# A rebuilt prologue: input order, a power on GpSimd, selection products, one exchange for the median

## The reference

```python
x = x + g(xn) * xn            # xn = _gn(x): 32 groups of 16 channels, normalised
# with xf = xn as (b, c, 256)
mean, mx, std = xf.mean(-1), xf.max(-1), xf.std(-1, ddof=1)
u   = stack([mean, mx, std], axis=-1)           # (8, 512, 3)
med = median(u.reshape(b, -1), axis=-1)         # one median of 1536 values per image
z   = einsum('bck,ck->bc', (u - med) ** 3, cfc_w) / sqrt(1 + 1e-5) * bn_w + bn_b
g   = sigmoid(z)
```

## Time and profile before

| | before |
|---|---|
| median of 3 runs | 725.55 us |
| profiled execution, its own time | 728.12 us |
| span of the profile | 726.4 us |
| PE busy | 646.2 us (89%) |
| DVE busy | 441.0 us (61%) |
| ACT busy | 336.2 us (46%) |
| POOL busy | 285.7 us (39%) |

### The profile page before, as it was taken

How to read it: one execution, slowest core, us unless ns; L and a number is a source line. 1 busy time by engine, 2 the same in 40 slices (tenths; PEclk the granted TensorE clock), 3 DMA queues, 4 the chain that set the end, 5 groups by cost and what they waited for, 6 DMA issues and landing times.

```text
span 726.4 us, 14162 instructions
## 1 busy us (share of the span) xinstructions
PE 646.2 (89%) x4944; PEld 543.8 (75%) x4945; DVE 441.0 (61%) x974; ACT 336.2 (46%) x616; POOL 285.7 (39%) x329
## 2 busy tenths in 40 slices
PE   0213989999999999999999999999899999999992
PEld 0203978888888888888689899999687878878881
DVE  7775344756565656573645996233567677767771
ACT  8641254646464646464634223434444544544440
POOL 1340153434343434342421113865454554545524
PEclk9999999999999999999999999999999999999996
DMA  9800000101010101020025433352856556555543
GB/s 309 328 0 0 1 2 1 60 2 58 0 58 0 58 0 58 0 73 16 31 86 234 131 117 117 116 173 73 302 90 114 95 107 110 98 110 103 103 70 43
DMA packets 24786, 62.61 MB, mean 86 GB/s; under 512 B 3056, under 2 KB 7920, under 8 KB 23216
## 3 DMA queue, kind: packets, MB, share of 16 engines
q1 hardware_dynamic: 14912, 41.69, 16.0%
q0 software_dynamic: 9168, 20.45, 15.5%
q10 hardware_dynamic: 672, 0.03, 0.1%
HBM read 39.09 MB, written 23.07 MB: 86 GB/s over the span
## 4 chain that ended last, share of the span: by engine, by line
PE 59%; DMA 26%; DVE 7%; issue 3%; POOL 3%; ACT 1%; SPq 0%; DVEq 0%; POOLq 0%; ACTq 0%
PE PS L1554 25%; DMA out_tokens<-yo,dest 24%; PE scores L1554 12%; PE PS L1663 6%; PE scores L1826 5%; PE scores L1649 3%; PE PS L1614 2%; DMA T<-in_x 1%; PE PS L1603 1%; DMA out_tokens<-yo,dest_halves 1%; DVE front L1034 1%; DVE qT L960 1%; POOL w_l L528 1%; PE PS L1690 1%; DVE qT L961 1%
## 5 line engine op out<-in xcount | busy, mean ns | idle before, releaser
L1554 PE MATMUL scores<-xb,sw_h 128*128 128x256 f32 x512 | 94.2, 284 | 0.0
L647 POOL DMA_INDIRECT out_tokens<-yo,dest x36 | 57.5, 1598 | 79.1 <-DMA out_tokens<-yo,dest 77.3
L1554 PEld LDWEIGHTS scores<-xb,sw_h 128*128 128x128 f32 x512 | 80.9, 191 | 2.3 <-ACT probs L745 0.4
L1554 PE MATMUL PS<-xt_h,w_h 128*128 128x256 f32 x256 | 76.2, 298 | 1.5 <-DVE xt_l L1176 1.5
L552 POOL TENSOR_SCALAR_AFFINE_SELECT probs<-probs 128x256 f32<-128x256 f32 x128 | 52.0, 432 | 57.6 <-ACT probs L749 56.8
L1554 PE MATMUL PS<-xt_l,w_h 128*128 128x256 f32 x256 | 73.9, 289 | 0.0
L1554 PE MATMUL PS<-xt_h,w_l 128*128 128x256 f32 x256 | 73.7, 288 | 0.0
L1554 PE MATMUL scores<-xb,sw_l 128*128 128x256 f32 x256 | 72.3, 282 | 0.0
L1191 DVE RECIPROCAL rden<-PS 128x256 f32<-128x256 f32 x32 | 56.2, 1755 | 24.8 <-PE PS L1663 24.8
L1554 PE MATMUL scores<-wgu_h,xgT_h 128*128 x156 | 64.8, 416 | 2.0 <-DVE xgT_l L1516 2.0
L745 ACT ACTIVATE probs<-scores 128x768 f32<-128x768 f32 x64 | 51.4, 802 | 26.8 <-PE scores L1649 26.7
(11 more groups left out here) (297 smaller groups left out, 1597.1 us busy)
## 6 DMA issues: line engine op xcount, KB each, us to landing
wgu_l<-in_wgu SPq DMA_DIRECT2D x8, 1024.0 KB, 6.6
T<-in_x SPq DMA_DIRECT2D x8, 512.0 KB, 7.7
w_in<-in_wqkvo SPq DMA_DIRECT2D x4, 1024.0 KB, 12.5
x_rows<-x SPq DMA_DIRECT2D x8, 512.0 KB, 2.8
x_cols<-x2T SPq DMA_DIRECT2D x8, 512.0 KB, 2.6
xc<-x_cols SPq DMA_DIRECT2D x8, 512.0 KB, 3.3
out_tokens<-T SPq DMA_DIRECT2D x8, 512.0 KB, 7.5
wd_sb<-in_wd SPq DMA_DIRECT2D x8, 512.0 KB, 7.0
```

Of the source, the lines that this page charges most:

```text
L647: pool.indirect_dma_start(out[:, :], bass.IndirectOffsetOnAxis(dest[:, t:t + 1], 0), yo[:, t % 3, :], None, compute_op=ALU.add).then_inc(y ...
L1554: ins = pe.matmul(out, lhs(k, a), rhs(k, b), start=m == 0, stop=m == len(products) - 1)
```

## The change

- The images are loaded, and DVE takes their statistics, in the order 0, 1, 4, 2, 5, 3, 6, 7. ACT works in two groups, images 0 and 1 and then 2 and 3, each with its sums, scaling and squares.
- ACT's square root and the five DVE instructions behind it go. POOL raises both variances to a power in one instruction (128x64, exponents -0.5 and 0.5). DVE forms u with three small instructions.
- u is widened to 16 columns for each image (the spare ones hold a large number) and transposed in one piece; DVE copies the transposed matrix from PSUM. Twelve float32 products with a 0/1 matrix `selection`, which POOL fills ahead of the power, put the values where the twelve transposes put them.
- The last steps of the median are done in one exchange: each partition finds the least value at or above `low`, the greatest up to a bound `high`, the least above it, and a count; one product brings the four to 8 rows, a second one spreads the median.
- The coefficients take fewer instructions: the two channel weights are multiplied beforehand, and one over (1 + exp) is taken together with the deviation.
- ACT applies the coefficients to two of the four pieces of image 0.
- PE gets products whose result nobody reads (`keep_busy`): 10 before the group means, 8 before the transpose of u, 9 before the transposes of image 0 and 16 behind them.
- POOL's low parts of the weights no longer wait for `spread_full`.

```diff
+UM = 16
+ARRIVAL = (0, 1, 4, 2, 5, 3, 6, 7)
...
+        exponents = kf[:, 20 * n32:22 * n32]
+        deviation = kf[:, 22 * n32:23 * n32]
+        u_wide = vf[:, 0:B * UM]
+        u = u_wide.rearrange("p (b n) -> p b n", b=B)[:, :, 0:UP]
+        uw = vf[:, B * UM:B * UM + 3 * B * UP].rearrange("p (k n) -> p k n", k=3)
+        uT = vf[:, 416:416 + P]
...
-            for b in range(B):
+            for b in ARRIVAL:
...
+            pool.tensor_copy(selection.rearrange("p (n b j) -> p n b j", n=UP, b=B),
+                             ident[:, :].rearrange("p (b n) -> p n b", b=B)[:, 0:UP, :].unsqueeze(3).to_broadcast(
+                                 [P, UP, B, THRESHOLDS])).then_inc(selection_ready, 1)
+            pool.wait_ge(var_ready, 1)
+            pool.tensor_tensor(root, var2, exponents, ALU.pow).then_inc(root_ready, 1)
...
+            for first, group in enumerate(((0, 1), (2, 3))):
+                these = [(b, k, CB * b + k) for b in group for k in range(CB)]
+                lo, hi = CB * group[0], CB * (group[-1] + 1)
+                for b, k, c in these:
+                    act.wait_ge(x_loaded[b], 16)
+                    ins = act.activation(unread[c], at(T, b)[:, k * S:(k + 1) * S], ACT.Copy,
+                                         accum_out=small[:, 12, c:c + 1])
+                ins.then_inc(act_sums, 1)
...
-            act.wait_ge(var_ready, 1)
-            act.activation(root, var2, ACT.Sqrt).then_inc(root_ready, 1)
...
+            act.wait_ge(coef_ready, 1)
+            for k in (2, 3):
+                ins = act.activation(front[:, k * S:(k + 1) * S], at(T, 0)[:, k * S:(k + 1) * S], ACT.Identity,
+                                     bias=coefB[:, k:k + 1], scale=coefA[:, k:k + 1])
+            ins.then_inc(y0_upper, 1)
...
-            dve.wait_ge(dve_step, step_of(dve.reciprocal(inv2, root)))
-            dve.wait_ge(dve_step, step_of(dve.tensor_tensor(root2, var2, inv2, ALU.mult)))
-            dve.wait_ge(dve_step, step_of(dve.tensor_tensor(root2, root2, root, ALU.add)))
-            dve.wait_ge(dve_step, step_of(dve.reciprocal(inv2[:, 0:n32], root2[:, 0:n32])))
-            r = inv2[:, n32:2 * n32]
-            dve.wait_ge(dve_step, step_of(dve.tensor_scalar(r, inv2[:, 0:n32], 2.0, None, ALU.mult)))
-            u3 = u.rearrange("p (n k) -> p n k", k=UK)
-            def spread_out(k):
-                return every_u[k].rearrange("p (c b j) -> p b c j", c=CB, b=B)
-            def every(t):
-                return t.rearrange("p (b c) -> p b c", b=B).unsqueeze(3).to_broadcast([P, B, CB, THRESHOLDS])
-            dve.tensor_tensor(spread_out(0), every(K(7)), every(r), ALU.mult).then_inc(every_ready, 1)
-            dve.tensor_tensor(spread_out(1), every(K(10)), every(r), ALU.mult).then_inc(every_ready, 1)
-            dve.tensor_tensor(spread_out(2), every(root2[:, n32:2 * n32]), every(inv2[:, 0:n32]),
-                              ALU.mult).then_inc(every_ready, 1)
-            dve.tensor_tensor(u3[:, :, 0], K(7), r, ALU.mult)
-            dve.tensor_tensor(u3[:, :, 1], K(10), r, ALU.mult)
-            dve.scalar_tensor_tensor(u3[:, :, 2], root2[:, n32:2 * n32], 0.5, r, ALU.mult, ALU.mult).then_inc(u_ready, 1)
+            by_b = "p (b n) -> p b n"
+            r = root[:, 0:n32]
+            u4 = u.rearrange("p b (c k) -> p b c k", k=UK)
+            def per_batch(t):
+                return t.rearrange(by_b, b=B)
+            dve.wait_ge(dve_step, n.value())
+            dve.tensor_tensor(u4[:, :, :, 0], per_batch(K(7)), per_batch(r), ALU.mult)
+            dve.tensor_tensor(u4[:, :, :, 1], per_batch(K(10)), per_batch(r), ALU.mult)
+            dve.tensor_tensor(u4[:, :, :, 2], per_batch(root[:, n32:2 * n32]), per_batch(r),
+                              ALU.mult).then_inc(u_ready, 1)
...
+            dve.wait_ge(uT_full, 1)
+            dve.tensor_copy(uT, PS[6][:, 0:P]).then_inc(uT_ready, 1)
+            dve.wait_ge(uT_ready, 1)
...
+            size_step = step_of(dve.scalar_tensor_tensor(low_size, low, -1.0, low, ALU.mult, ALU.max))
+            from_low = step_of(dve.tensor_scalar(least_of[:, 0, :], uT, low, BIG, ALU.is_lt, ALU.mult))
+            dve.wait_ge(dve_step, size_step)
+            dve.wait_ge(dve_step, step_of(dve.tensor_scalar(low_size, low_size, 3.0 / 2 ** 23, WIDTHS[-1], ALU.mult,
+                                                            ALU.add)))
+            high_step = step_of(dve.tensor_tensor(high, low_size, low, ALU.add))
+            step_of(dve.tensor_tensor(least_of[:, 0, :], least_of[:, 0, :], uT, ALU.add))
+            dve.wait_ge(dve_step, high_step)
+            counted = step_of(dve.tensor_scalar(least_of[:, 2, :], uT, high, 0.0, ALU.is_le, ALU.add,
+                                                accum_out=cols[:, 3:4]))
+            over_high = step_of(dve.tensor_scalar(least_of[:, 1, :], uT, high, BIG, ALU.is_gt, ALU.mult))
+            dve.wait_ge(dve_step, counted)
+            step_of(dve.scalar_tensor_tensor(least_of[:, 2, :], least_of[:, 2, :], BIG, uT, ALU.mult, ALU.add))
+            dve.wait_ge(dve_step, over_high)
+            dve.wait_ge(dve_step, step_of(dve.tensor_tensor(least_of[:, 1, :], least_of[:, 1, :], uT, ALU.subtract)))
+            dve.wait_ge(dve_step, step_of(dve.tensor_reduce(cols[:, 0:3], least_of, AX.X, ALU.min)))
+            dve.tensor_tensor(cols_of, cols.unsqueeze(2).to_broadcast([P, 4, UM]),
+                              own_slot.unsqueeze(1).to_broadcast([P, 4, UM]), ALU.mult).then_inc(med_in, 1)
...
+            by_slot = PS[4][0:B, 384:384 + 4 * UM].rearrange("p (k j) -> p k j", k=4)
+            at_low, minus_high, over, count, apart, second, both = [rows[:, k:k + 1] for k in range(7)]
+            dve.wait_ge(dve_step, step_of(dve.tensor_reduce(count, by_slot[:, 3, :], AX.X, ALU.add)))
+            step_of(dve.tensor_reduce(rows[:, 0:3], by_slot[:, 0:3, :], AX.X, ALU.min))
+            dve.wait_ge(dve_step, step_of(dve.tensor_scalar(apart, count, MED_N / 2 + 0.5, BIG, ALU.is_lt, ALU.mult)))
+            dve.wait_ge(dve_step, step_of(dve.scalar_tensor_tensor(second, at_low, apart, over, ALU.add, ALU.min)))
+            dve.wait_ge(dve_step, step_of(dve.tensor_tensor(both, second, minus_high, ALU.subtract)))
+            dve.tensor_scalar(diagonal, ident[0:B, 0:B], both, 0.5, ALU.mult, ALU.mult).then_inc(med_in, 1)
...
-                uw[:, 0, :].rearrange(by_b, b=B), uw[:, 2, :].rearrange(by_b, b=B),
-                prm[:, 0:UP].unsqueeze(1).to_broadcast([P, B, UP]), ALU.mult)))
-            dve.wait_ge(dve_step, step_of(dve.tensor_reduce(
-                K(11), uw[:, 0, :].rearrange("p (n k) -> p n k", k=UK), AX.X, ALU.add)))
-            bn_scale = float(1.0 / np.sqrt(np.float32(1.0) + np.float32(EPS)))
-            dve.wait_ge(dve_step, step_of(dve.scalar_tensor_tensor(
-                K(12).rearrange(by_b, b=B), K(11).rearrange(by_b, b=B), bn_scale,
-                prm[:, UP:UP + CB].unsqueeze(1).to_broadcast([P, B, CB]), ALU.mult, ALU.mult)))
...
+            squared = step_of(dve.tensor_tensor(uw[:, 1, :], uw[:, 0, :], uw[:, 0, :], ALU.mult))
...
+                uw[:, 2, :].rearrange(by_b, b=B), uw[:, 0, :].rearrange(by_b, b=B),
+                weights3.unsqueeze(1).to_broadcast([P, B, UP]), ALU.mult)))
...
+            dve.wait_ge(dve_step, step_of(dve.scalar_tensor_tensor(K(0), K(15), 1.0, deviation, ALU.add, ALU.mult)))
+            dve.wait_ge(dve_step, step_of(dve.reciprocal(K(2), K(0))))
             step_of(dve.tensor_scalar(coefA[:, :], K(2), 1.0, None, ALU.add))
-            dve.wait_ge(dve_step, step_of(dve.scalar_tensor_tensor(
-                coefB[:, :], grp_mean, -1.0, K(2), ALU.mult, ALU.mult)))
+            dve.scalar_tensor_tensor(coefB[:, :], grp_mean, -1.0, K(2), ALU.mult, ALU.mult).then_inc(coef_ready, 1)
...
-                for k in range(CB):
+                for k in range(2 if isinstance(b, int) and b == 0 else CB):
...
+            def keep_busy(times):
+                for _ in range(times):
+                    pe.matmul(PS[3][:, 384:512], ident[:, :], ident[:, :], start=True, stop=True)
+            pe.wait_ge(consts_done, NCONSTS)
+            pe.wait_ge(x_loaded[B - 2], 16)
+            keep_busy(10)
...
+            keep_busy(8)
+            pe.wait_ge(u_ready, 1)
+            pe.transpose(PS[6][:, 0:P], u_wide, ident[:, :]).then_inc(uT_full, 1)
+            pe.wait_ge(selection_ready, 1)
+            pe.wait_ge(uT_ready, 1)
...
+                ins = pe.matmul(spread_u[q // (UP // 2)][:, at_q:at_q + P], selection[:, q * P:(q + 1) * P], uT,
+                                start=True, stop=True)
...
+            pe.matmul(PS[4][0:B, 384:384 + 4 * UM], own_batch, cols_of.rearrange("p k j -> p (k j)"), start=True,
+                      stop=True).then_inc(med_out, 1)
...
+            pe.matmul(PS[6][:, 0:B], ones[0:B, :], diagonal, start=True, stop=True).then_inc(med_out, 1)
...
+            keep_busy(9)
             y_transposes("lead", 0, 0)
```

(32 more changed lines are left out.)

141 lines of the change are left out of this document (44 added, 97 removed).

## The result

The changed kernel takes 737.56 us (median of 6 runs, 736.42 to 739.93), the kernel before 725.77 on the same chip (6 runs, 724.23 to 728.19). The ratio is 1.0162, with an interval of 1.0137 to 1.0188: slower by 1.6%, where 720.9 us were forecast. The profiled execution took 737.16 us, its span is 735.4.

A forecast was written before the change was run, and what follows sets the result against it. Step latency was taken to bound the prologue, and PE to be full from the first projection on. Terms -1.0 + 2.8 - 2.8 - 0.65 - 0.45 - 2.6 = -4.7 us on 725.55 gave 720.9; range 715.5 to 727.5.

The forecast's parts named there:

- From the variances to the first round: Prologue from the variances to the first count: 8.5 us instead of 5.65, so 2.8 us more than before.
- the products: Twelve float32 products with `selection` on PE ahead of the rounds: 4.0 us, between 2.8 and 5.3 by the clock.
- The power: POOL's 128x64 power on the path to u: 3.0 us, the geometric middle of 0.7 and 13.1.
- Rival D: POOL's power goes by column, 13.1 us on the path: +6.8 us, 732.3 us; deciding from 10 us on; chance 0.08.
- The low pieces beside DVE: POOL's low parts of the weights, now started before the rounds, beside DVE instructions: contention noted, nothing added.
- the counts: DVE's counts in the rounds beside POOL's low parts: they read PSUM, so nothing added; eight rounds of 2.17 us unchanged.
- The median: Exchange of the median after the rounds: 5.7 us instead of 8.5, a gain of 2.8 us.
- the coefficients: Coefficients after the median: three instructions fewer on the path and one square overlapped, a gain of 0.65 us.
- The affine: Affine pieces of image 0, two on ACT at 0.4 to 0.5 us each: 1.0 us instead of 1.39, gain 0.45.
- The order of x: Image order in DVE's statistics: the last maximum ends at 20.0 us instead of 21.0, a gain of 1.0 us.
- Hidden up to 16 us: POOL's filling of `selection` between 4 and 21 us: hidden, at no cost, up to 16 us of work.
- The clock: PE's clock, raised by unread products, at first transposes, second transposes and first projections: 2.6 us credited of 4.2 possible.

The follow-up runs named there:

- e9: e5 with five more powers of 4 to 64 columns on POOL, results unread, run once for its profile: 732.74 us.
- e2: Changed kernel with the root back on ACT with five DVE instructions and the low pieces waiting: 725.10 us, 0.9936 of the kernel before.
- e1: Changed kernel with POOL's low pieces waiting again for the end of the twelve products, power kept: 734.44 us, 1.0064 of the kernel before.
- e3: e2 with POOL's low pieces started as soon as ACT's root is there: 734.22 us, 1.0054 of the kernel before.
- e12: e1 with five more small DVE instructions beside the power, results unread, run once for its profile: 733.81 us.
- e4: Kernel before with one line changed, POOL's low pieces started when the root is there: 739.26 us, 1.0116 of the kernel before.
- e5: e2 with POOL's copy into `selection` moved behind DVE's first constants: 726.19 us, 0.9909 of the kernel before.
- e11: e5 unchanged, measured again beside e10: 724.53 us, 0.9914 of the kernel before.
- e7: e5 with only the 9 and 16 unread products behind the median kept: 726.64 us, 0.9921 of the kernel before.
- e8: e5 with the images in the old order 0 to 7: 725.93 us, 0.9925 of the kernel before.
- e10: e5 with 6 more unread products between the second transposes and the projections, other counts slightly shifted: 725.96 us, 0.9929 of the kernel before.
- e6: e5 without any of the unread products: 727.49 us, 0.9936 of the kernel before.

## Why the prediction was wrong

**The step that failed** is "From the variances to the first round", forecast at 8.5 us and measured at 24.76. Of the 16.3 us between them 15.8 are two errors, and each has its runs; 0.3 more are the products, at 4.27 for 4.0.

*The power, 7.6 us.* I took 3.0 where it is 10.59, inside my bounds of 0.7 and 13.1. The middle was argued from what a long routine might overlap; the surplus of 0.4 us on two columns was the only measurement, and half of it, 0.2 us a column, was closer than my value (0.158, e9). e2 against e1 shows 9.3 us for the power against ACT's root. Rival D had this mechanism, and its point, from p = 10 on, is met; but I gave it 0.08. The sum with p = 10.59 and nothing else changed is -4.7 + 7.6 = +2.9 us. e1, which has just this, gives +4.2, of which 1.3 are its products at 5.34 us instead of 4.0.

*The low pieces beside DVE, 8.2 us, priced at nothing.* This is a wait that the sum did not have. I saw that "POOL's low parts now start before the rounds" and weighed them against the counts, which read PSUM. That part holds: L1056 takes 1.02 to 1.03 us beside the low pieces at 50.14, as in the rounds without them. But the pieces start with the power's end, together with the three instructions that form u, and I did not price those. Three at 2.3 us instead of 0.2 are 6.5; the fourth makes the copy 1.7 later. The Trainium skill (GPSIMD Engine Reference, 8) says that GpSimd and DVE contend where a DVE instruction has two SBUF inputs or is in a 2-port perf mode; it gives no size. The trace agrees: all four have two SBUF inputs, and each waits for a whole POOL instruction. Whether the one-input TENSOR_SCALAR of e3 (1.83 us) was in such a mode no trace here shows; beside the power two inputs did not wait (e9, e12). e1, e3 and e4 show the cost three times, at 7.6, 9.1 and 9.0 us, in three different prologues. Neither error alone makes the measured result: e1 is the power alone (+0.64%), e3 the pieces alone (+0.54%). Over e2, which has neither (-0.64%), they are 1.3% and 1.2%; together from there that would be +1.8%, and +1.6% was measured.

**The other terms** were right or small. The median gained 3.7 for 2.8 and the coefficients 0.64 for 0.65. The affine gained 0.2 for 0.45: ACT's two pieces end at 74.20 (I put them at 0.4 to 0.5 us each, they take 0.54), and the nine unread products, at the low level throughout, at 74.47, so the transposes wait some 0.2 us for them. The order of x gained 0.45 for 1.0. "Hidden up to 16 us" was wrong of `selection`: it held a conversion at 4.01 for 1.3 us, of which 0.2 reach the end (e5). Most of the rest is the third image, which came at 8.31 in e5 and not at 8.02. The clock gave all of the 4.2 us in this execution, where I credited 2.6; e5 and e11 show that it is not given every time, and that part of it can go at the next pause. Which of the two this execution would show was luck. That the clock column before "reads 0.50 only at 97 to 100 us" was misread: it is down at 356 to 360 us too (0.52 and 0.62); nothing in the sum hangs on it.

With both errors out the rest of the sum holds in size. e2 is 5.2 us faster than before by the medians (interval of the ratio 0.9915 to 0.9956, so 3.2 to 6.2 us); the forecast was 4.7. That its first count is at 31.91, where 31.8 was forecast, is luck: the variances end 1.25 us late there (24.55 for 23.3), and the step behind them takes 7.36 us for 8.5, since ACT's root and its five instructions take 2.1 us where the sum has 3.1 up to u, and the products take 3.21 for 4.0. The clock also gave e2 more than the 2.6 of the sum: its 96 projections take 11.74 us. e5's kernel, measured twice, has the lowest ratios: 0.9909 and 0.9914, about 6.5 us below before and 2.5% below the changed kernel's ratio. The intervals of e2, e7, e8 and e10 overlap them.

**Still open:** what in POOL's instructions holds DVE; how much each group of unread products is worth in the whole time (e6, e7 and e10 differ by less than their intervals); and why the clock falls at one pause in one execution and at another in the next.

## What to carry to other kernels

When a step is moved off an engine, look at what stood behind its old wait: here the low pieces, not the power alone, came to lie beside the path. A large subtraction on POOL beside a chain of small products and sums on DVE turned each into one as long as POOL's. Of an operation seen at one small size, put its surplus in the sum as a price by the column until a second size says otherwise: that gave 13.1 us for the 10.59 measured, and the middle gave 3.0.
